# Re-timing the steps behind the attention of a two-layer gated cross-attention and mixture-of-experts kernel

## The reference

```
x = x + tanh(g_xattn[0]) * L0_attention(layernorm(x), ctx, group_prob, mask)
x = x + tanh(g_ffn[0])   * L0_experts(layernorm(x))
x = x + tanh(g_xattn[1]) * L1_attention(layernorm(x), ctx, mask)
x = x + tanh(g_ffn[1])   * L1_experts(layernorm(x))
```

## Time and profile before

| | us |
|---|---|
| median of 3 runs | 926.21 (925.9 to 927.81) |
| the profiled execution, its own time | 927.88 |
| its span, first to last instruction | 926.1 |
| busy PE / DVE / ACT / POOL | 784.4 / 688.7 / 609.3 / 546.6 |
| attention of layer 0 (scores of slot 0 to 127) | 35 to 264 |
| tail of layer 0 until the first expert's transpose | 264 to 304 |
| experts of layer 0 | 304 to 435 |
| attention of layer 1 | 436 to 695 |
| experts of layer 1 | to 926 |

### The profile page before, as it was taken

How to read it: one execution, slowest core, us unless ns; L and a number is a source line. 1 busy time by engine, 2 the same in 40 slices (tenths; PEclk the granted TensorE clock), 3 DMA queues, 4 the chain that set the end, 5 groups by cost and what they waited for, 6 DMA issues and landing times.

```text
span 926.1 us, 20429 instructions
## 1 busy us (share of the span) xinstructions
PE 784.4 (85%) x6554; PEld 618.1 (67%) x6554; DVE 688.7 (74%) x1980; ACT 609.3 (66%) x2582; POOL 546.6 (59%) x798
## 2 busy tenths in 40 slices
PE   2698999888964899998877788888978889999996
PEld 1366666666742799987555556656756768888885
DVE  5688899999987334454988799999887666666664
ACT  2498899889852445444976779799987444444442
POOL 6266578888677002031668887465324867777775
PEclk9999999999995799999987889999999999999998
DMA  6999975576248433225328365654100000000000
GB/s 165 242 268 242 261 244 145 120 172 155 57 108 300 126 108 96 71 80 122 80 65 160 101 126 133 147 121 125 47 14 23 24 23 24 24 23 13 12 1 23
DMA packets 85139, 101.68 MB, mean 110 GB/s; under 512 B 8448, under 2 KB 70853, under 8 KB 84360
## 3 DMA queue, kind: packets, MB, share of 16 engines
q1 hardware_dynamic: 80936, 92.13, 38.9%
q0 software_dynamic: 4096, 8.25, 3.6%
HBM read 63.32 MB, written 45.99 MB: 118 GB/s over the span
## 4 chain that ended last, share of the span: by engine, by line
PE 40%; DVE 25%; ACT 16%; issue 10%; POOL 8%; DMA 1%; SPq 0%; POOLq 0%; DVEq 0%; ACTq 0%
ACT exp L856 12%; PE psum L699 7%; DVE shift L1041 5%; PE psum L739 5%; PE psum L741 5%; PE psum L740 5%; DVE exp_T L1051 2%; PE psum L687 2%; DVE ln_stats L1023 2%; DVE exp_T L1053 2%; PE psum L688 2%; PE psum L689 2%; POOL scratch_xe L1568 2%; POOL got_rows L1587 2%; PE psum L582 2%
## 5 line engine op out<-in xcount | busy, mean ns | idle before, releaser
L856 ACT ACTIVATE exp<-psum,shift 128x120 f32<-128x120 f32 x1024 | 367.3, 441 | 72.8 <-DVE shift L1041 72.3
L856 ACT ACTIVATION_READ_ACCUMULATOR exp<-psum,shift 128x1 f32 x1024 | 276.2, 286 | 0.0
L569 PE MATMUL psum<-ident,exp 128*120 128x128 f32 x1024 | 162.3, 282 | 33.0 <-DVE exp_T L1053 18.0
L1041 DVE TENSOR_REDUCE shift<-psum 128x4 f32<-128x480 f32 x256 | 165.6, 648 | 28.6 <-PE psum L560 27.6
L1422 DVE SCALAR_TENSOR_TENSOR q_operand<-psum,comb,q_operand 128x256 f32<-128x256 f32 x256 | 111.5, 479 | 73.7 <-ACT q_operand L988 73.7
L1657 POOL TENSOR_TENSOR q_operand<-q_operand 128x512 f32<-128x512 f32 x96 | 126.4, 1317 | 58.7 <-DVE q_operand L1422 53.4
L569 PEld LDWEIGHTS psum<-ident,exp 128*120 128x120 f32 x1024 | 117.5, 141 | 52.5 <-DVE exp_T L1053 23.4
L988 ACT ACTIVATE q_operand<-psum 128x512 f32<-128x512 f32 x128 | 76.2, 599 | 114.7 <-PE psum L741 114.6
L1587 POOL DMA_INDIRECT got_rows<-scratch_y,slot_get x64 | 67.1, 1048 | 123.7 <-DMA scratch_y<-y_rows 107.2
L557 PE MATMUL psum<-neg_rows,const_bf 128*128 128x480 bf16 x256 | 98.0, 383 | 39.0 <-ACT exp L856 28.3
L560 PE MATMUL psum<-k_operand,q_operand 128*128 128x240 bf16 x512 | 97.3, 273 | 0.0
(11 more groups left out here) (175 smaller groups left out, 1669.8 us busy)
## 6 DMA issues: line engine op xcount, KB each, us to landing
k_operand<-scratch_k SPq DMA_DIRECT2D x32, 360.0 KB, 6.9
q_operand<-scratch_q SPq DMA_DIRECT2D x30, 384.0 KB, 6.4
scratch_q<-parts SPq DMA_DIRECT2D x15, 384.0 KB
scratch_k<-parts SPq DMA_DIRECT2D x14, 360.0 KB, 4.4
scratch_xe<-in_zero_rows SPq DMA_DIRECT2D x8, 512.0 KB, 8.5
scratch_y<-in_zero_rows SPq DMA_DIRECT2D x8, 512.0 KB, 6.7
scratch_q<-parts SPq DMA_DIRECT2D x15, 256.0 KB
scratch_k<-parts SPq DMA_DIRECT2D x14, 240.0 KB, 4.0
```

Source lines behind the costliest of these rows:

```text
L569: ins = pe.transpose(ps[0:S2, T_BANKS[G % 2], u * S:(u + 1) * S], atts[l].expS[:, G % RING_E, u, :], ident[:, :])
L856: ins = act.activation(atts[l].expS[:, G % RING_E, u, :], ps[:, S_BANKS[G % 3], u * S2:(u + 1) * S2], ACT.Exp, bias=atts[l].shift[:, i % 2 ...
L1041: dve.tensor_reduce(atts[l].shift[:, i % 2, 4 * r:4 * r + 4], ps[:, S_BANKS[G % 3], 0:4 * S2].rearrange("p (h k) -> p h k", h=4), AX_X, AL ...
```

## The change

No arithmetic is added or dropped. Steps move between slots, and two sums change engine. The new table NEXT0 is used for chunk 6 of layer 0; TIGHT0 now for chunks 4, 5 and 7. In layer 0 `powers` now goes ahead of all other steps of its slot on POOL.

```diff
-MID1 = dict(k_project=6, k_take=7, k_part0=8, k_left0=9, k_part1=9, k_left1=10, k_out=(10, 12, 14), k_fetch=24,
-            stat=15, power=15, norm=17, turn=18, turned=19, bias=30,
-            q_project=21, q_take=22, q_part0=23, q_left0=23, q_part1=24, q_left1=24, q_out=(24, 25, 26), q_fetch=28)
+MID1 = dict(k_project=6, k_take=7, k_part0=8, k_left0=9, k_part1=9, k_left1=10, k_out=(10, 12, 14), k_fetch=1,
+            stat=13, power=13, norm=15, turn=18, turned=19, bias=30,
+            q_project=21, q_take=22, q_part0=22, q_left0=23, q_part1=24, q_left1=24, q_out=(24, 25, 26), q_fetch=28)
@@ bring_slot
-    return {8: 0, 9: 7, 10: 9, 11: 11}[i] if c == 2 else {3: 13, 4: 21, 5: 29, 6: 37, 7: 52}[c] + 2 * b
+    return {8: 0, 9: 2, 10: 4, 11: 7}[i] if c == 2 else {3: 11, 4: 20, 5: 29, 6: 37, 7: 52}[c] + 2 * b
@@ add_y_slot
-        return {6: 6, 7: 6, 8: 11, 9: 13, 10: 14, 11: 15, 12: 21, ...
+        return {6: 6, 7: 6, 8: 10, 9: 11, 10: 12, 11: 13, 12: 21, ...
@@
-TIGHT0 = dict(stat=0, power=1, norm=4, turn=6, turned=7, gate=10, logits=13, top=13, one_hot=13, exp=14,
+TIGHT0 = dict(stat=0, power=0, norm=4, turn=6, turned=7, gate=10, logits=13, top=13, one_hot=13, exp=14,
               ranks=15, take_ranks=17, positions=17, slots=17, send=18)
+NEXT0 = dict(stat=0, power=0, norm=4, turn=5, turned=6, gate=8, logits=10, top=10, one_hot=10, exp=11,
+             ranks=11, take_ranks=13, positions=13, slots=13, send=14)
@@ post_at
-    return POST if j < 5 else TIGHT0 if l == 0 else TIGHT6 if j == NCH - 2 else TIGHT
+    return POST if j < 5 - (l == 0) else (NEXT0 if j == NCH - 2 else TIGHT0) if l == 0 else TIGHT6 if j == NCH - 2 else TIGHT
@@
-SPLIT_KEYS_AT = {5: (0, 1), 8: (2,), 19: (3, 4, 5)}
+SPLIT_KEYS_AT = {5: (0, 1), 19: (2, 3, 4, 5)}
@@ vector_program, behind: scale_bo1 at slot 37 for 36
@@ vector_program, expert1, after the gating of the unit
+            if w == UNITS - 1:
+                m = (PAIRS_E - 1) * i + p - 1
+                on.wait_ge(f_gated, 2 * w + 2)
+                on.wait_ge(f_sum, m)
+                dve.tensor_tensor(acc[:, i % R_ACC, :], acc[:, i % R_ACC, :], ga[:, m % R_GA, :], ALU.add).then_inc(f_sum, 1)
+                on.wait_ge(f_sum, m + 1)
+                on.wait_ge(f_turn, i - 1)
+                dve.tensor_tensor(total[:, i % 2, :], acc[:, i % R_ACC, 0:HID1], acc[:, i % R_ACC, HID1:2 * HID1], ALU.add).then_inc(f_total, 1)
@@ gpsimd_program, behind: one_mask at slot 116 for 124; the powers of all chunks ahead of the chunks' other steps
@@ gpsimd_program, expert1
+            if w == UNITS - 1:
+                return
@@ sync_program, behind: the load of mask1 at slot 110 for 120, the loads of vbo and vo at slot 31 for 24
```

More of the change, by code:

```diff
@@ L190, in add_y_slot @@
     if c < 6:
-        return {6: 6, 7: 6, 8: 11, 9: 13, 10: 14, 11: 15, 12: 21, 13: 22, 14: 23, 15: 24, 16: 29, 17: 30, 18: 31, 19: 32,
+        return {6: 6, 7: 6, 8: 10, 9: 11, 10: 12, 11: 13, 12: 21, 13: 22, 14: 23, 15: 24, 16: 29, 17: 30, 18: 31, 19: 32,
                 20: 38, 21: 39, 22: 40, 23: 41}[i]
@@ L1263, in behind @@
                     add_y(i)
-            if l == 1 and s == 36:
+            if l == 1 and s == 37:
                 scale_bo1()
@@ L1620, in behind @@
                 less_last((s - LAST_AT) // LAST_EVERY)
-            if l == 0 and s == 124:
-                one_mask()
             if l == 0 and s % 16 == 2 and s // 16 + 1 < NCH:
                 masks(s // 16 + 1)
+            if l == 0 and s == 116:
+                one_mask()
+            for j in range(NCH):
+                if s - after_slot(j) == post_at(l, j)["power"]:
+                    powers(1, l * NCH + j)
             for j in range(NCH):
                 o = s - after_slot(j)
-                if o == post_at(l, j)["power"]:
-                    powers(1, l * NCH + j)
                 if o == post_at(l, j)["norm"] and (l == 1 or j < ON_DVE):
@@ L1834, in behind @@
                     load_group(s // 16 + 1)
-            if l == 0 and s == 120:
+            if l == 0 and s == 110:
                 sp.dma_start(mask1[:], t["mask1"]).then_inc(mask_in, 16)
@@ L1838, in behind @@
                 clear_spares(0, SPOILT)
-            if l == 1 and s == 24:
+            if l == 1 and s == 31:
                 sp.dma_start(vbo[:], t["f1_bo"].partition_broadcast(S)).then_inc(ld_bo1, 16)
```

## The result

The changed kernel is slower, and by nearly five times what was forecast: 941.49 us median of 4 runs (939.8 to 942.1), beside 926.06 (924.28 to 927.81) for the kernel before, ratio 1.0161 with a 95% interval of 1.0146 to 1.0177. That is +15.4 us; the forecast was +3.2 and its range ended at 932.5. The profiled execution took 939.8 us (span 938.0), so the two spans differ by 11.9 only. Lines of the changed kernel are 3 to 14 higher than before: L506 for L503, L1517 for L1506, L1579 for L1568, L1044 for L1041. In e2, e6 and e12 most are 3 higher still (L509, L1520, L1582).

A forecast was written before the change was run, and what follows sets the result against it. DVE was taken as the fullest engine in layer 0's attention, ACT close, with POOL's time at the wrong place. Layer 0 +5.4, layer 1 -1.3 and last unit -0.9 gave +3.2 us: 929.4, range 921.0 to 932.5.

The forecast's parts named there:

- I count none of it in the end: Layer 0, slot 97: PE's stop for chunk 4's normalisation, 1.5 to 5 us, covered by DVE's waiting in slots 105 and 106.
- What is given back: Layer 0, slot 114: chunk 4's positions are gone from there, giving back 0.6 us.
- Nothing is taken away there: POOL ahead of chunk 5's normalisation: chunk 4's `slots` and three sends are added, so it ends at 244.4 for 236.0.
- My upper bound: Layer 0's attention: 7.7 us, if ACT's and DVE's delay of slot 98 reaches POOL before slot 108, another 1.7.
- The loss at slot 114: Layer 0: slot 114 late by 6.6 us, as PE waits for POOL's normalisation of chunk 5.
- The tail, -0.6: Layer 0 after the attention: logits of chunk 7 gain 1.2 us, later powers cost 0.6; bounds -1.7 to +1.5.
- +0.6 for the powers: Layer 0's tail: chunk 7's powers now stand behind the first two sends of chunk 6, costing 0.6 us.
- Layer 1, -1.3: Layer 1, chunk 2: slot 32's wait goes, slot 37's stays, slot 38 comes 1.3 us sooner; bounds -4.6 to +2.
- the fetch of k beside the first gathers: Layer 1's upper bound, +2 us, with denser slots 10 to 15; a rival with blocked adds, 933, chance 0.08.
- both sides cancel: Rival: layer 0 at its low bound, layer 1 at -2.5, the last unit -0.9, giving 926.2; chance 0.15.
- The last unit, -0.9: The end: POOL's third sum and fold, 2.05 us, become 1.18 on DVE; -0.9 us, bounds -1.1 and -0.4.
- The rule weighed: Layer 1's adds of gathered rows and POOL's SBUF-reading instructions exclude each other; up to 7.6 us worse, given a small chance.

The follow-up runs named there:

- e2: The changed kernel with layer 0 chunk 4's `slots` at slot 112 and its sends from 113, its transposes staying at slot 97; 939.43 us, ratio 1.0144.
- e6: The changed kernel with the edits of e5 and e2 together: powers behind the sends and chunk 4's sends from slot 113; 931.30 us, ratio 1.0057.
- e12: The changed kernel with powers behind sends, chunk 4's transposes at slot 99, sends from 113, chunk 6's from 141, layer 1's k fetched at slot 12; 929.85 us, ratio 1.0040.
- e5: The changed kernel with POOL's powers of chunks 4 to 7 back behind the sends of their slot, all else kept; 939.63 us, ratio 1.0140.
- e1: The changed kernel with layer 0's chunk 4 alone back on its former table (transposes at slot 103, sends from 117); 932.98 us, ratio 1.0086.
- e8: The kernel before with the edits of layer 1, but chunk 2's k fetched at slot 12 instead of 1; 926.29 us, ratio 0.9989.
- e4: The kernel before with only the edits of layer 1 (k fetched at slot 1, gathers of chunk 2 at 0 to 8); 928.11 us, ratio 1.0018.
- e3: The kernel before with only the last unit's two sums moved from POOL to DVE; 924.64 us, ratio 0.9979.
- e11: The kernel before with the last sum of the two last units and the last fold on DVE; 924.72 us, ratio 0.9980.

## Why the prediction was wrong

**The direction was right and its place too; two terms of layer 0's attention failed.** It was put at +6.0 us and lost 12.3. Of the 6.3 us between, the slots from 97 to 113 hold 4.75 (put at nothing) and those from 114 to 127 hold 1.7 (put at -0.6, measured +1.09). Slot 114 itself has none of it.

- *The step that failed: "I count none of it in the end", of the stop at slot 97.* The terms of this step were good: a start of the normalisation at 210.8, measured 212.11, of which 1.2 us were lost before slot 97; an end at 212.5, measured 213.85 with the same 1.2. What failed is the cover: of the 4.52 us lost at slot 98 nothing had come back at slot 113. DVE's waits in slots 105 and 106 are indeed gone, but the same edit moved chunk 4's routing into slots 104 to 108. DVE is busy for 19.86 of 20 us there in after (the line below), for 18.15 of 20 in the same slots before (218 to 238). e5 shows it with a short stop: 1.57 lost at slot 98, 2.33 by slot 113. Of the 4.52 us the order of the powers makes 3; the rest is chunk 4's earlier place (e5, e1).

```profile
223.00:243.00 20.00, 17.25 (x212) 12.84 (x210) 19.86 (x69) 16.94 (x95) 14.27 (x27) 1.00 0.58 130
```

- *"What is given back": 0.6 us, from chunk 4's positions.* At slot 115 DVE had 0.38 of it. At slot 116 it was 1.1 us later again, because PE came out of its stop at the low clock and kept it for some 5 us: its projection ahead of that slot took 1.38 us for 0.97. In e5 the clock was back sooner (0.86 in 247.3 to 248.5, while after has 0.59 in 253.0 to 254.8), and that slot lost nothing. PE's timeline in after, then in e5:

```profile
253.68 1.38 PE L528 MATMUL psum<-ctx_T,wk 128*128 128x480 f32 x2
```

```profile
248.37 0.97 PE L528 MATMUL psum<-ctx_T,wk 128*128 128x480 f32 x2
```

- *"Nothing is taken away there", with chunk 5's normalisation at an end of 244.4.* I had worked out in the paragraph before that the powers of chunk 4 go ahead of two sends, and did not carry the same edit on to chunk 5. Where nothing else stands there this is worth 3.97 us at slot 114 (e1). In the changed kernel it is worth 0.9 (e5), so it is not what the forecast missed. The end came at 249.35, of which 1.2 us were lost before slot 97. From the end of chunk 4's normalisation to that of chunk 5's POOL took 35.50 us for 25.45 before: 10.0 more, where I had 6.4. The difference is waits: 2.32 for ACT (0.46 before), 1.31 for DVE's statistics and 0.55 for DVE's routing. DVE had been late since slot 98; the wait for ACT stands in e5 too, behind its shorter stop, and isn't explained further. My upper bound had such a delay of POOL, at 1.7 us. POOL's timeline before, then in after:

```profile
219.03 1.08 POOL L1519 TENSOR_TENSOR full<-full,parts 128x480 f32<-128x480 f32 x1 [0.46 <-ACT parts L828]
```

```profile
224.58 1.09 POOL L1530 TENSOR_TENSOR full<-full,parts 128x480 f32<-128x480 f32 x1 [2.32 <-ACT parts L831]
```

- *The loss at slot 114.* Forecast 6.6, measured 6.50, and this hit is luck: the normalisation ended 4.95 us later than I had it and PE came to it 4.8 us later, 1.2 of each being lost ahead of slot 97. Slot 98's loss, kept by all engines, moved both.
- *The powers of the chunks ahead.* The edit puts the powers first for every chunk of layer 0, not only from chunk 4 on, and I gave the others nothing. Between slots 65 and 97 after lost 0.8 us, e1 1.1 and e2 0.8; all other kernels, whose powers stand behind the sends, stay within 0.04 of before.
- *The tail, -0.6.* Measured +0.29. Counted from slot 127's maxima, the powers of chunk 7 started 3.4 us later than before (291.44 for 274.56), its normalisation 2.1 (293.50 for 277.91), its logits 0.9 (298.50 for 284.09), the last send 0.5 (313.23 for 299.18). The mis-sized term is "+0.6 for the powers", for which I gave no row: it was 2.1 at the normalisation. That of `split_keys` was right, 1.2 us less from normalisation to logits (5.0 for 6.2).
- *Layer 1, -1.3.* Up to slot 127 it was +0.3. The waits at slots 32 and 37 went as forecast. What I gave 0.8 us was 4.15 at slot 7: the sums of row pairs 6 and 7 waited for their gathers. It was the upper bound's cause ("the fetch of k beside the first gathers") that came true, as e8 against e4 shows. The chance of 0.08 for it was too small, but its price was not kept: e8 without this wait is as far behind at slot 14. (In the rival "both sides cancel", -2.5 isn't the middle of a range from -4.6 to +2; that is -1.3. The forecast doesn't use it.)
- *The last unit, -0.9.* The chain as such: first sum of POOL to PE's transposes 5.27 us before and 4.33 in after, -0.94. The end moved by 2.2. It kept its distance of 6.2 us from POOL's last instruction, and that came sooner by as much.
- *The rule weighed.* The adds of gathered rows that I feared would be blocked: in 448 to 545 the 18 first adds took 335, 345 and 1908 ns (min, median, max) for 339, 344 and 1289. The median is the same and none of the loss hangs on them. But the traces tell the cause of the long ones. Of all adds of gathered rows in layer 1, first and second, 8 took over 0.8 us in before and 9 in after. Each of these 17 ran beside a POOL instruction with two inputs (1.15 to 1.4 us) and ended 0.14 to 0.16 us after it. The 19 and 13 adds beside which POOL did nothing but issue gathers took at most 0.41 us. So the rule holds in this kernel, but not for the gathers, beside which the four adds were moved. DVE's and POOL's timeline before:

```profile
522.20 1.29 DVE L1156 SCALAR_TENSOR_TENSOR x_rows<-got_rows,slot_weight,x_rows 128x128 f32<-128x128 f32 x1
```

```profile
522.18 1.16 POOL L1529 TENSOR_TENSOR parts<-full,parts 128x512 bf16<-128x512 f32 x1
```

The rest of the 15.4 us: single stretches up to slot 127 of layer 1 sum to 12.3 + 0.3 + 0.3, and the end to -2.2, 10.7 in all; 1.2 lie ahead of slot 97, 0.5 of them already at slot 0, where nothing is edited, and most of the rest is the powers of the chunks ahead. The 3.5 us between the two spans' difference and the medians' are of the size of what slots 37 to 56 gave in that execution, and e3's had them too without an edit there. Which executions have them, and why, stays open.

The landing that the old order hid is what the Trainium skill ("DMA: Bandwidth & Descriptors", Rules for kernel authors) asks for: issue the transfer early, compute, and wait late. This case's trace agrees: the powers, 3.2 us of arithmetic, stood between the send and the wait, and with them moved POOL waited 1.64 us in after, 2.04 in e1 and 3.47 in e2.

## What to carry to other kernels

Slack seen further down covers a stop only if the same change moves no work into it; that is what failed here. An edit of a shared table or loop is to be worked through for every chunk that reads it, not for the one in view: two copies of a move already understood were overlooked, one worth 0.8 us ahead of slot 97, one 0.9 at slot 114, where it would have been 4 without chunk 4's sends. On an engine that issues transfers, a piece of arithmetic between the last send and the step that reuses its buffer isn't free to go ahead: it is the cover of the landing.

## What the runs showed of the hardware

- **The end came 6.2 us after POOL's last instruction.** The span ended 6.2 us after POOL's last instruction in before (919.87 to 926.1), in after (931.77 to 938.0) and in eleven of the twelve experiments, whereas from DVE's last instruction it was anything from 2.0 to 3.6. Only in e11, with POOL done 7.4 us ahead, was it DVE's end plus 2.0. What fills the 6.2 us isn't in the records, so that the end hangs on POOL is inferred from this distance, not seen.
- **A stop costs at its end too.** Behind PE's waits of 3.10 and 6.82 us the granted clock fell, and the same four transposes took 1.09 us for 0.66. Behind waits of 3.50 (e1), 3.99 (e2) and 5.94 us (e5) they took 1.08 to 1.09 too. Behind waits of 1.57 (e5, e6) it stayed at 1.00 and they took 0.63. The windows of after behind slot 98, and before and behind slot 114 (PEclk is the third column from the end):

```profile
214.00:218.00 4.00, 4.00 (x20) 3.12 (x21) 2.04 (x6) 1.97 (x9) 3.76 (x6) 0.63 0.20 75
...
243.00:249.40 6.40, 0.00 (x0) 0.00 (x0) 0.85 (x2) 2.14 (x13) 5.29 (x11) 0.86 0.09 31
249.40:256.00 6.60, 6.50 (x30) 4.90 (x31) 3.66 (x8) 4.09 (x18) 5.15 (x8) 0.61 0.12 41
```

  From the transposes' start to slot 114's maxima it was 1.10 us at a clock of 1.00 (238.99 for 237.89) and 1.92 at the low level, 1.2 GHz (251.42 for 249.50): 0.8 of the 6.5 us, and slot 116 was 1.1 us later on top. That idling drops TensorE to 1.2 GHz is what the Trainium skill says ("TensorE: Matmul & The Clock Gate", What's actually happening), and the trace agrees.
- **A VectorE sum with two SBUF inputs can be held by a POOL sum.** All 17 long adds of gathered rows (0.89 to 2.09 us, for a usual 0.35) ended 0.14 to 0.16 us after a two-input POOL instruction; the 32 beside gathers alone took at most 0.41 us (above, "The rule weighed").
- **A send's landing is no constant.** From the start of the send to the step that waited for it: 2.6 us in after, 3.0 in e1, 4.45 in e2.
